# Softmax attention: scores one unit nearer to the row maxima, maxima turned right after their negation, two of four stores begun by GpSimd

## The reference

```python
x = L0_attn_a_x                                   # (1, 2048, 128)
xn = layernorm(x)
keys, queries, values = xn @ triu(Wk).T, xn @ tril(Wq).T, xn @ Wv.T      # each as 16 heads of 8
dot = einsum('bqhs,bkhs->bhqk', queries, keys) / sqrt(8)                 # 2048 x 2048 per head
out = einsum('bhqk,bkhs->bqhs', softmax(dot, axis=-1), values)
x = x + out @ Wu.T + bu
...                                               # seven more layers
```

## Time and profile before

| | |
|---|---|
| Time before, median of 3 runs | 1618.25 us (1617.51 to 1619.01) |
| Profiled execution, its own time | 1618.27 us |
| Span from its first to its last instruction | 1616.6 us |
| Busy: PE / DVE / ACT / POOL | 1480.8 / 1359.2 / 937.9 / 295.8 us |
| The 512 row maxima (L874) | 585.6 us |
| Negations (L860), first and last start | 66.6 and 627.0 us |

### The profile page before, as it was taken

One profiled execution on the slowest core, in us unless ns is written; L12 is line 12 of the kernel. 1 busy time (PEld: TensorE's weight loads), 2 busy tenths in 40 slices (PEclk: granted clock), 3 DMA queues, 4 the chain that ended last, 5 costly groups with the idle time before them and its releaser, 6 DMA issues. The chain is left out here.

```text
span 1616.6 us, 27627 instructions
## 1 busy us (share of the span) xinstructions
PE 1480.8 (92%) x10285; PEld 766.2 (47%) x10285; DVE 1359.2 (84%) x2459; ACT 937.9 (58%) x1768; POOL 295.8 (18%) x352
## 2 busy tenths in 40 slices
PE   7999999999999999799998888876999969989699
PEld 2122222222222222388873333323888858769587
DVE  7999999999999999376665999998766768787686
ACT  3188999999999999632236665754322342222232
POOL 4200000000000000000015878873000200020000
PEclk8599999999999999899998999999999979999799
DMA  3340110000000001000002222110000012300123
GB/s 112 117 139 25 32 33 32 25 25 25 25 25 25 25 27 56 3 1 1 1 1 66 66 65 72 68 65 20 1 1 1 1 38 70 107 1 1 54 84 102
DMA packets 41328, 66.13 MB, mean 41 GB/s; under 512 B 11444, under 2 KB 18661, under 8 KB 40490
## 3 DMA queue, kind: packets, MB, share of 16 engines
q1 hardware_dynamic: 41194, 64.37, 12.6%
HBM read 56.68 MB, written 6.75 MB: 39 GB/s over the span
## 5 line engine op out<-in xcount | busy, mean ns | idle before, releaser
L874 DVE TENSOR_REDUCE row_max<-ps 128x1 f32<-128x1024 f32 x512 | 585.6, 1216 | 19.4 <-PE ps L659 19.0
L780 ACT ACTIVATE probs<-ps 128x512 f32<-128x512 f32 x944 | 505.7, 596 | 60.1 <-PE ps L674 43.9
L659 PE MATMUL ps<-k_stack,q_stack 48*128 48x512 bf16 x1024 | 325.1, 403 | 8.7 <-DVE row_max L874 3.0
L600 PE MATMUL ps<-probs,v_head 128*16 128x256 f32 (+1 forms) x3800 | 315.3, 404 | 6.3 <-issue 6.3
L674 PE MATMUL ps<-q_stack,k_stack 51*128 51x512 bf16 x944 | 288.3, 386 | 3.5 <-DMA q_stack<-max_dram 2.8
L1400 PE MATMUL ps<-s_hc,ident 128*128 128x512 f32 x256 | 139.0, 628 | 48.6 <-DVE s_hc L1673 43.5
L1053 ACT ACTIVATE x_gate<-ps 128x512 f32<-128x512 f32 x128 | 76.5, 599 | 183.3 <-PE ps L122 183.2
L659 PEld LDWEIGHTS ps<-k_stack,q_stack 48*128 48x128 bf16 x1024 | 60.2, 95 | 255.3 <-DVE row_max L874 233.0
L1325 POOL TENSOR_TENSOR s_dbx<-s_dx,s_b_rows 128x512 f32<-128x512 f32 x128 | 159.4, 1269 | 35.7 <-DVE s_h L1664 35.1
L1664 DVE TENSOR_TENSOR_SCAN s_h<-ps,s_state,s_dbx 128x512 f32<-128x512 f32 x128 | 157.0, 1269 | 4.5 <-POOL s_dbx L1325 2.8
L600 PEld LDWEIGHTS ps<-probs,v_head 128*16 128x16 f32 x3800 | 62.6, 94 | 202.8 <-issue 102.4
(11 more groups left out here) (351 smaller groups left out, 1943.8 us busy)
## 6 DMA issues: line engine op xcount, KB each, us to landing
s_b_rows<-s_b_dram SPq DMA_DIRECT2D x64, 256.0 KB, 3.1
y_spread<-y_probs_dram SPq DMA_DIRECT2D x128, 128.0 KB, 3.0
q_stack<-q_parts_dram SPq DMA_DIRECT2D x30, 96.0 KB
k_stack<-k_parts_dram SPq DMA_DIRECT2D x30, 96.0 KB
w_w<-w_dram SPq DMA_DIRECT2D x1, 2048.0 KB, 7.8
q_stack<-q_parts_dram SPq DMA_DIRECT2D x30, 64.0 KB
k_stack<-k_parts_dram SPq DMA_DIRECT2D x30, 64.0 KB
o_dram<-o_sb SPq DMA_DIRECT2D x60, 32.0 KB
```

The costliest lines, as they stand in the source:

```text
L600: last = nc.tensor.matmul(core.ps[32 * c:32 * c + VROWS, O_BANK, cut], v_head[buf][:, kt, :], probs[:, m % RING, c * CH:(c + 1) * CH][:, cut],
L659: last = nc.tensor.matmul(core.ps[:, 2 * b + r, :], qst[buf][0:KROWS, u * P:(u + 1) * P], kst[buf][0:KROWS, key:key + CH], start=True, sto ...
L780: nc.scalar.activation(probs[:, us % RING, c * CH:(c + 1) * CH], core.ps[:, S_BANK + n % S_RING, :], ACT.Exp).then_inc(exp_done, 1)
L874: nc.vector.tensor_reduce(mx[:, head % 2, u, b:b + 1], core.ps[:, 2 * b:2 * b + 2, :], mybir.AxisListType.XY, ALU.max).then_inc(max_done, 1)
```

## The change

`LAG_S` becomes 19, so that each score, and with it the values, comes one slot earlier with respect to the maxima, and 19 units remain for the tail. `turn_max` follows `negate_max` directly in every head. Of the four stores of the cut maxima, SyncE begins the first two, and GpSimd the last two right after its cut, with a semaphore of their own; SyncE waits for both pairs before the load, and GpSimd waits for both before it overwrites the parts. `TAIL_BANKS` is rotated to go with the new lag.

```diff
@@ -268,7 +268,7 @@
     QPARTS = ((0, 3), (0, 2), (0, 1))
     KTIMES = (3, 2, 1)
     RING = 4
-    LAG_S = NT + 4
+    LAG_S = NT + 3
     LAG_V = LAG_S + 2
     NBUF = 3
     BODY = NBUF * NT
@@ -276,7 +276,7 @@
     S_BANK, S_RING, O_BANK = 4, 3, 7
     UNITS = HEADS * NT
     TAIL = UNITS - LAG_S
-    TAIL_BANKS, EARLY_OUT_BANK, LAST_TILES = (6, 4, 5, 0, 1, 2), 3, 3
+    TAIL_BANKS, EARLY_OUT_BANK, LAST_TILES = (4, 5, 6, 0, 1, 2), 3, 3
     OUT_UNITS = range(UNITS - 2 * NC_ + 1, UNITS)
     VROWS = 2 * HD
     with ExitStack() as ctx:
@@ -342,6 +342,7 @@
         nm_line = core.sem("a_nm_line")
         nm_ready = core.sem("a_nm_ready")
         m_stored = core.sem("a_max_stored")
+        m_stored_low = core.sem("a_max_stored_low")
         m_loaded = [core.sem(f"a_max_loaded{i}") for i in range(NBUF)]
         v_staged = core.sem("a_v_staged")
         s_done = core.sem("a_scores")
@@ -420,10 +421,11 @@
             def store_max(head, par):
 
                 sp.wait_ge(nm_ready, head + 1)
-                for b in range(P // 32):
+                for b in range(2):
                     sp.dma_start(md[par].rearrange("p (j b i) -> b j p i", b=P // 32, i=32)[b],
                                    nm_parts[32 * b:32 * b + NT, :, :]).then_inc(m_stored, 16)
-                sp.wait_ge(m_stored, (head + 1) * 64)
+                sp.wait_ge(m_stored, (head + 1) * 32)
+                sp.wait_ge(m_stored_low, (head + 1) * 32)
                 sp.dma_start(qst[par][HALF + KROWS:ROWS, :], md[par]).then_inc(m_loaded[par], 16)
                 if head >= HEADS - 2:
                     sp.dma_start(qst[par][KROWS:KROWS + NPART, :], md[par]).then_inc(low_loaded[head % 2], 16)
@@ -511,7 +513,8 @@
 
                 pool.wait_ge(nm_turned, head + 1)
                 if not isinstance(head, int) or head:
-                    pool.wait_ge(m_stored, head * 64)
+                    pool.wait_ge(m_stored, head * 32)
+                    pool.wait_ge(m_stored_low, head * 32)
                 round_to(nm_parts[:, 0, :], nmT[:]).then_inc(nm_line, 1)
                 pool.wait_ge(nm_line, head * 3 + 1)
                 nc.gpsimd.tensor_tensor(nm_parts[:, 1, :], nmT[:], nm_parts[:, 0, :], ALU.subtract).then_inc(nm_line, 1)
@@ -519,6 +522,10 @@
                 pool.wait_ge(nm_line, head * 3 + 3)
                 nc.gpsimd.tensor_tensor(nm_parts[:, 2, :], nm_rest[:], nm_parts[:, 1, :],
                                         ALU.subtract).then_inc(nm_ready, 1)
+                pool.wait_ge(nm_ready, head + 1)
+                for b in range(2, P // 32):
+                    nc.gpsimd.dma_start(md[head % NBUF].rearrange("p (j b i) -> b j p i", b=P // 32, i=32)[b],
+                                        nm_parts[32 * b:32 * b + NT, :, :]).then_inc(m_stored_low, 16)
 
             for head in range(NBUF):
                 stage_v(head, head)
@@ -876,7 +883,6 @@
                         if head and u == 0:
                             if b == 0:
                                 negate_max(head - 1)
-                            else:
                                 turn_max(head - 1)
             negate_max(HEADS - 1)
             turn_max(HEADS - 1)
```

## The result

The changed kernel takes 1636.09 us (median of 4 runs, 1632.62 to 1637.52), the kernel before in the same comparisons 1617.88 us. The ratio is 1.0109, with a 95% interval of 1.0097 to 1.0122: 17.6 us slower (the two medians lie 18.2 us apart). The forecast was slower by 41.5 us; the median lies in its range of 1620 to 1692. The profiled execution took 1637.52 us.

What follows compares the result with a forecast made beforehand. VectorE's maxima were taken to set the pace. Heads 3 to 14 +35.9, heads 0 to 2 +5.6, tail nothing: +41.5 on 1618.27 gives 1659.8 us; range 1620 to 1692.

Steps and rivals of the forecast that it cites:

- The chain from the negation to the first score: Head boundary: negation, turn, GpSimd's cut, stores, load, first score; before the change it arrives about 0.1 us before needed.
- lateness is paid in full: Head boundary: a late first score lengthens the head's period by its lateness (head 9: 0.56 late, 0.54 longer).
- the unit saved in the tail: Tail after the last maximum: 19 units of scores left, not 20; at most 1.98 us gained, forecast nothing.
- x: Time from GpSimd's last cut to the landing of its second store; taken as 3.45 us.
- e: Lengthening of a head by its late first score, VectorE's 0.13 hidden in it; taken as 1.86 us.
- second rival: Head boundary: both queues issue alike, GpSimd's stores land later; +8.6 to +16.9 us, 1626.9 to 1635.2; chance 0.22.
- two stores on GpSimd: Head boundary: 1.01 us for each store, one behind the other, then the median landing of 1.4 us.
- 12 x 1.13 = 13.6 for the clock: Heads 3 to 14: TensorE's standstill halves the granted clock; 1.5 us in three heads of four, 1.13 a head.
- their slow landings stay: Heads 0 to 2: already late, they pay only the later score, 3 x 1.86 = 5.6 us.
- Three heads of four: Heads 3 to 14: share in which about 1.45 us of TensorE standing still costs 1.5 us of clock.
- The 0.13 us for the turn: VectorE at the head boundary: turn directly behind the negation holds it 0.13 us more, 2.0 us in 15 heads.
- SyncE's half: Head boundary: SyncE's two stores land 1.84 us after the cut; this half alone makes the score 0.25 late.

## Why the prediction was right and wrong

*Right: the direction and its mechanism.* The chain from the negation to the first score decides, lateness is paid in full, and the unit saved in the tail is never collected. With the measured x of 2.49 the prediction's own e = x - 1.59 is 0.90; the quiet head pays 0.83. The second rival, "late by tenths" with x between 2.0 and 2.8, is what happened; I gave it 0.22. That the median of 1636.09 lies 1 us above that rival's upper end, 1635.2, is not the rival's arithmetic: with x = 2.49 the prediction's own sum is 15 x 0.90 = 13.5, less 0.93 from the tail, +12.6. The profiled heads and tail cost 16.6: heads 5 to 14 7.9 instead of 9.0, heads 0 to 4 8.8 instead of 4.5, the tail gave 0.1 instead of 0.9.

*Wrong: the term "two stores on GpSimd".* I took x = 0.03 + 2 x 1.01 + 1.4, the 1.01 from GpSimd's power, as "a program's price". Measured are 0.30 until the first is begun, 0.57 and 0.51 for the two (1.08 together), and 1.11 from the end of the second to the last landing: 2.49. The price of a store lies at half of my value, nearer to the 0.43 that SyncE takes for the same bytes than to GpSimd's power. And a part of the landing was counted twice: the 1.4 of the earlier trace rows runs from an issue's begin, and I set it behind the end. Nor was it 48 pieces: the profile lists SyncE's store as 48 packets of 64 bytes, GpSimd's as 16 of 192 (and 16 of 4 bytes with either). That this makes it cheaper is not shown. In the changed kernel SyncE's and GpSimd's stores land 1.4 and 1.7 us after their begins (columns: KB each, median us):

```profile
max_dram<-neg_max_parts SPq DMA_DIRECT2D x32, 3.0 KB, 1.4
...
max_dram<-neg_max_parts POOLq DMA_DIRECT2D x32, 3.0 KB, 1.7
```

What hangs on this term: 12 x 1.86 = 22.3 should have been 12 x 0.9 = 10.8, and the 12 x 1.13 = 13.6 for the clock should have been nothing in the ten heads 5 to 14, where standstills of 0.41 to 0.54 left the clock at 1.00. The kernel with four stores on GpSimd puts the error back in: its heads 5 to 14 cost 29.7 against the 29.9 of the forecast, so the other terms of these heads were not far off together.

The Trainium skill's figure for the first byte, 1 us against 0.6 ("DMA: Bandwidth & Descriptors", "Latency and other measured facts"), agrees with the trace in its difference: in head 8 the first packets start 1.15 us after GpSimd's begin and 0.82 after SyncE's, 0.33 apart. By the Trainium skill's difference of 0.4 alone x would be 2.24; 2.49 was measured.

*Wrong in size, and not seen: heads 0 to 4.* I took "their slow landings stay" for heads 0 to 2 and a quiet price for 3 and 4. The slow landings were no property of the early heads. In the ten profiled executions shown here, 160 boundaries, the wait from cut to load is over 0.15 us longer than its kernel's median 47 times; in 46 of these a packet of instructions was under way between the cut and the usual landing. Of the 113 others 13 had one. Part of the mechanism shows in the single packets: in 29 of the 47 a store's packets pause for 0.15 us or more and go on 0.003 to 0.015 us before a packet of instructions ends, as in head 3; in none of the 113. There a part of a store went on only when the packet was through; for the other 18, and for the longer landing after the last packet, the cause stays open. The lag moves these packets against the stores: heads 3 and 4 meet one in all five kernels with lag 19 and in none of the five with lag 20. They cost 8.3 us of the 16.7, of which 1.7 is the quiet price.

*The clock.* Three heads of four was too many for quiet heads: with lag 19 alone and 1.8 us of standing still it fell in five of nine, with four stores on GpSimd and 1.4 to 1.6 us in four of seven.

*The rest.* The 0.13 us for the turn was exact (36.99). In the changed kernel SyncE's half is not the last to land. And the prediction gave the turn at once no worth of its own: with it alone the stores of heads 1 and 2 have landed by N+4.4, before their packets of instructions start (N+4.94 and N+5.41), which saves 5.8 us for 2 us of VectorE.

## What to carry to other kernels

Read the slack of a chain before its distance is cut: here 0.1 us of slack and a chain shortened by 1.27 stood against a distance shortened by 2.27, and even with GpSimd's stores at SyncE's price the score would have come 0.25 late by the prediction's sum. Price an operation that the trace doesn't show by the nearest row of the same kind (here the same transfer on another engine), not by the nearest program of the same engine, and keep begin, end and landing apart. A shorter chain at the old distance was the better use: the turn at once alone took 1615.3 us where the kernel before took 1618.9, a gain of 0.2%.

## What the runs showed of the hardware that I had not expected

Two small stores cost GpSimd 0.57 and 0.51 us to begin, and their landing after the end of the issue (1.11) is near that of SyncE's (1.02). A packet of instructions of 8 or 16 KB (0.3 to 1.4 us for one) beside small stores goes with loads that begin up to 2.25 us later; in 29 of 47 such heads packets of the store resume 0.003 to 0.015 us before it ends. A shift of the program by one unit decides which heads meet it. Two standstills of TensorE of the same length, 1.82 and 1.81 us, left the granted clock at 1.00 in one head and at 0.50 in the next.
